# Scattering edge rows into a rank table: positions outside a pass go to spare rows by a clamp

## What is computed

```python
row = edge_index[0]                                   # src, 400000 node numbers
seg_sum = segment_sum(edge_attr, row, num_segments=N) # N = 12500, 32 features
seg_max = segment_max(edge_attr, row, num_segments=N)
cnt = segment_sum(ones, row, num_segments=N)
seg_mean = seg_sum / maximum(cnt, 1.0)
seg_max = where(cnt > 0, seg_max, 0.0)
h = concatenate([seg_sum, seg_max, seg_mean, u[batch]], axis=1)   # 97 columns
h = relu(h @ W1 + b1)                                 # 128 columns
x = x + (h @ W2 + b2)                                 # 64 columns
```

## Time and profile before

| | us |
|---|---|
| median of three runs (4393.61 to 4400.94) | 4397.47 |
| the profiled execution | 4387.55 |
| its span | 4385.8 |
| busy in the span: PE / DVE / ACT / POOL | 2956.9 / 2990.5 / 1416.7 / 3106.0 |

### The profile page before, as it was taken

How to read it: one execution, slowest core, us unless ns; L and a number is a source line. 1 busy time by engine, 2 the same in 40 slices (tenths; PEclk the granted TensorE clock), 3 DMA queues, 4 the chain that set the end, 5 groups by cost and what they waited for, 6 DMA issues and landing times.

```text
span 4385.8 us, 87474 instructions
## 1 busy us (share of the span) xinstructions
PE 2956.9 (67%) x18710; PEld 2189.1 (50%) x18710; DVE 2990.5 (68%) x12042; ACT 1416.7 (32%) x4649; POOL 3106.0 (71%) x3144
## 2 busy tenths in 40 slices
PE   5677667776666666666666677777777777677554
PEld 3455446654444444444444466666655555466443
DVE  7577559974444555545444589988888888589664
ACT  3333332233333333333333333333343333322133
POOL 5777777777777777777777777777677777777500
PEclk9987558855555555555555588877767787578677
DMA  7899873311111111111111233333313332143232
GB/s 294 315 379 372 326 261 113 113 25 26 25 26 26 25 26 26 26 25 26 25 25 26 65 112 100 102 110 99 99 53 90 87 96 83 42 119 118 71 98 69
DMA packets 410044, 454.47 MB, mean 104 GB/s; under 512 B 65002, under 2 KB 381460, under 8 KB 409620
## 3 DMA queue, kind: packets, MB, share of 16 engines
q1 hardware_dynamic: 309876, 401.37, 27.9%
q0 software_dynamic: 100000, 51.40, 4.8%
HBM read 221.50 MB, written 231.02 MB: 103 GB/s over the span
## 4 chain that ended last, share of the span: by engine, by line
POOL 43%; issue 21%; DVE 19%; DMA 7%; PE 6%; POOLq 2%; DVEq 1%; SPq 1%; ACT 1%; ACTq 0%
POOL sorted_rows L441 43%; DVE peak_ps L801 5%; DVE raised L784 3%; DMA sorted_rows<-edges,position 3%; DVE picked L725 3%; PE misc_ps L528 2%; DMA edges<-in_edge_attr 2%; DVE lent L717 2%; DMA win<-sorted_rows 1%; POOLq L441 1%; DVE hot_owner L708 1%; PE start_ps L497 1%; DVE raised L812 1%; DVE peak_ps L779 1%; DVE rank_c L735 1%
## 5 line engine op out<-in xcount | busy, mean ns | idle before, releaser
L441 POOL DMA_INDIRECT sorted_rows<-edges,position x3125 | 3083.6, 987 | 1022.3 <-issue 949.5
L501 PE MATMUL place_ps<-start_sb,lent 98*128 98x128 bf16 x3125 | 875.6, 280 | 1033.3 <-DVE rank_f L725 1031.3
L612 ACT ACTIVATE start_sb<-start_ps 98x128 bf16<-98x128 f32 x3125 | 865.7, 277 | 1663.9 <-PE start_ps L497 804.6
L497 PE MATMUL start_ps<-hot_owner,hot_block 128*98 128x128 bf16 x3125 | 977.9, 313 | 144.5 <-ACT start_sb L612 105.6
L725 DVE CUSTOM_DVE_ANT_0 picked<-place_ps,hot_owner 128x128 bf16<-128x128 f32 x3125 | 886.9, 284 | 99.9 <-issue 62.9
L501 PEld LDWEIGHTS place_ps<-start_sb,lent 98*128 98x128 bf16 x3125 | 375.2, 120 | 1149.7 <-DVE rank_f L725 1116.5
L503 PE MATMUL place_ps<-hot_owner,lent 128*128 128x128 bf16 x3125 | 892.6, 286 | 0.0
L740 DVE SCALAR_TENSOR_TENSOR position<-rank_c,src_f 128x5 int32<-128x5 f32 x625 | 104.6, 167 | 1079.0 <-DMA sorted_rows<-edges,position 1031.1
L497 PEld LDWEIGHTS start_ps<-hot_owner,hot_block 128*98 128x98 bf16 x3125 | 460.3, 147 | 621.3 <-ACT start_sb L612 611.1
L474 PE MATMUL same_ps<-lent 98*128 98x128 bf16 x3125 | 651.5, 287 | 78.0 <-DVE lent L717 38.0
L528 PE MATMUL misc_ps<-win,ident_f 128*128 128x224 f32 x2548 | 701.2, 438 | 0.0
(11 more groups left out here) (79 smaller groups left out, 1413.4 us busy)
## 6 DMA issues: line engine op xcount, KB each, us to landing
sorted_rows<-zeros SPq DMA_DIRECT2D x110, 1568.0 KB, 26.2
win<-sorted_rows SPq DMA_DIRECT2D x56, 1344.0 KB
edges<-in_edge_attr SPq DMA_DIRECT2D x625, 80.0 KB
sorted_rows<-edges,position POOLq DMA_INDIRECT x3125
win<-sorted_rows SPq DMA_DIRECT2D x28, 1008.0 KB
win<-sorted_rows SPq DMA_DIRECT2D x14, 1680.0 KB
win<-sorted_rows SPq DMA_DIRECT2D x14, 1568.0 KB
win<-sorted_rows SPq DMA_DIRECT2D x14, 896.0 KB
```

Source lines behind the costliest of these rows:

```text
L441: nc.gpsimd.indirect_dma_start(out=rows[:, :], out_offset=bass.IndirectOffsetOnAxis(ap=position[:, t:t + 1], axis=0), in_=edges[:, k, j * ...
L497: nc.tensor.matmul(start_ps[0:BLOCKS, 0:P], hot_block[:, t, :], hot_owner[:, t, :], start=False, stop=False, skip_group_check=True).then_i ...
L501: nc.tensor.matmul(place_slot(j), hot_block_t[:, slot, j * P:(j + 1) * P], start_sb[:, j, :], start=True, stop=False)
L612: nc.scalar.activation(start_sb[:, j, :], start_ps[0:BLOCKS, 0:P], ACT.Copy)\
```

## The change

The segments' planes are laid out with one spare plane ahead of, between and behind them: `BASE` starts at 1 and each segment takes one plane more. `shift` starts at `BASE[s]` and not at zero, so that the running count, and with it `rank_f`, is the plane's number and not the rank in the segment. `make_positions` limits that number from both sides, to the spare plane ahead of the segment and the one behind it, in one operation; the next multiplies by the plane's size, adds the node number and converts. The scatter has no bound any more. `take_counts` takes the base off again while it copies. The table has 112 planes in place of 110; the number of fills stays.

```diff
-BASE = [sum(s[1] for s in SEGMENTS[:k]) for k in range(len(SEGMENTS) + 1)]
+BASE = [1 + sum(s[1] + 1 for s in SEGMENTS[:k]) for k in range(len(SEGMENTS) + 1)]
...
-                nc.gpsimd.memset(shift[:, s, :], 0.0).then_inc(const_made, 1)
+                nc.gpsimd.memset(shift[:, s, :], float(BASE[s])).then_inc(const_made, 1)
...
                                     out_offset=bass.IndirectOffsetOnAxis(ap=position[:, t:t + 1], axis=0),
-                                    in_=edges[:, k, j * FEAT:(j + 1) * FEAT], in_offset=None,
-                                    bounds_check=(BASE[s] + ranks[s]) * PLANE - 1, oob_is_err=False)\
+                                    in_=edges[:, k, j * FEAT:(j + 1) * FEAT], in_offset=None)\
                                     .then_inc(edges_sent[k], 16)
...
-                    nc.vector.scalar_tensor_tensor(rank_c[:, mine], rank_f[:, mine], -float(ranks[s]), rank_f[:, mine],
-                                                   ALU.mult, ALU.max).then_inc(rank_clamped, 1)
-                    dve.wait_ge(rank_clamped, m * 2 + 1)
-                    nc.vector.tensor_scalar(rank_c[:, mine], rank_c[:, mine], float(ranks[s]), float(PLANE),
-                                            ALU.min, ALU.mult).then_inc(rank_clamped, 1)
-                    dve.wait_ge(rank_clamped, m * 2 + 2)
+                    nc.vector.tensor_scalar(rank_c[:, mine], rank_f[:, mine], float(BASE[s] + ranks[s]),
+                                            float(BASE[s] - 1), ALU.min, ALU.max).then_inc(rank_clamped, 1)
+                    dve.wait_ge(rank_clamped, m + 1)
                     if not begin:
                         dve.wait_ge(edges_sent[slot], c * (16 * GROUP))
-                    nc.vector.scalar_tensor_tensor(position[:, mine], rank_c[:, mine], float(BASE[s] * PLANE),
+                    nc.vector.scalar_tensor_tensor(position[:, mine], rank_c[:, mine], float(PLANE),
                                                    src_f[:, bass.ds(at * CHUNK + slot * GROUP, GROUP)],
-                                                   ALU.add, ALU.add).then_inc(position_ready, 1)
+                                                   ALU.mult, ALU.add).then_inc(position_ready, 1)
...
-                    nc.vector.tensor_copy(left_t[:, :], count_ps).then_inc(left_step, 1)
+                    nc.vector.tensor_scalar(left_t[:, :], count_ps, -float(BASE[s]), None, ALU.add).then_inc(left_step, 1)
```

## The result

The changed kernel takes 4322.59 us (median of 4, 4319.87 to 4331.62) against 4396.31 for the kernel before on the same chip: ratio 0.9835, 95% interval 0.9818 to 0.9852, so 73.7 us less. The forecast was 30 less; the time lies inside the stated range of 4130 to 4400 and far outside the forecast's own range of 4350 to 4388. The profiled execution took 4319.87 us, its span is 4318.1: 67.7 less than the span before.

A forecast was written before the change was run, and what follows sets the result against it. POOL's scatters were taken to bound the kernel, with DVE late in three stretches. 4387.55 - 30 (DVE) with 0 for bound and small things gives 4357.5; 9.9 for the median makes 4367 us, range 4130 to 4400 (own range 4350 to 4388).

The forecast's parts named there:

- What sets the time: Scatter stage: POOL paces alone at 1.282 us per scatter, except about 51 us of starvation where DVE is late.
- Step (1): DVE making positions: L732 goes, which counts only in the three late stretches; -30 us, at most 34.1.
- the 0.201 us per group: DVE time saved by dropping L732: 166 ns for the operation and 35 ns of idle time ahead of it.
- Rival C: Late stretches: PE and edge loads are as late as DVE, so the time stays at 4397 us; chance 0.08.
- Step (2): Scatter at L441 without its bound: register move gone for nothing, scatter's own 977 ns unchanged; taken as 0.
- a fixed walk over 128 rows: Scatter on POOL: reason for expecting no gain, its time supposedly set by building the transfer's entries.
- rival B: Scatter on POOL gets dearer without the bound, by 19 ns, giving 4409 us; 14 ns decides; chance 0.11.
- my own sign: Wrong if the quiet stretch's period leaves 1.28 us by over 1%, or starvation of 2560 to 3250 stays at 30.
- The register move: POOL's sequencer at L441: 3125 moves of 29 ns, 91 us, disappear but gain nothing, since the sequencer is ahead.
- Rival A: Scatter on POOL gets shorter without the comparison: 90 ns gives 4174 us, 45 ns gives 4273; chance 0.25.
- Step (3): Small things taken at 0: base subtracted in the count copy (1.6 us in all), shift's memset, two more planes, no added wait.

The follow-up runs named there:

- e2: Changed kernel with a bound on the scatter again, at the end of the spare plane: 4350.74 us, ratio 0.9921 to the kernel before.
- e4: Kernel before without L732, the clamp of negative ranks; bound and register move stay: 4353.16 us, ratio 0.9922 to the kernel before.
- e1: Kernel before with only the scatter's bound taken away: 4368.22 us, ratio 0.9951 to the kernel before.
- e7: Changed kernel, without bound, each scatter sending 64 of the 128 rows; only the scatter's duration was read: 892 ns, against 967 with 128 rows.
- e3: Changed kernel with a bound at the table's end, from a register set once before the loops: 4349.02 us, ratio 0.9920 to the kernel before.
- e5: Changed kernel with an unused register move written ahead of each scatter, no bound; the moves did not run: 4323.09 us.
- e6: Kernel before with the limiting operation at L735 writing another tile than the one it reads: 4386.66 us, ratio 1.0000 to the kernel before.
- e9: Changed kernel without edit on the second chip: 4321.23 us, ratio 0.9853 to the kernel before on that chip.
- e11: Changed kernel without any clamp, the operation at L731 removed too: 4317.21 us, ratio 0.9838 to the kernel before.

## Why the prediction was wrong

**What sets the time: right.** POOL's 3125 scatters, each with a constant 0.305 us of idle time, paced the stage, and three late stretches starved for 51 us. Time was gained in both, in the scatter's own duration and in starvation.

**Step (1), DVE's operation: right in mechanism, the size a little low.** It was taken as -30, at most -34. Alone it gives 39 to 44 us of starvation and 37 to 46 us of the stage (e2 to e4). In the changed kernel starvation falls by 32.8 us only, because faster scatters starve sooner (e1: 51 to 54); that the fall of the idle time, 31.8 us, came out so near 30 is partly luck. The term that was too small is the 0.201 us per group: the 52 ns by which the next operation became shorter were not in it. I had the row with 225 ns for L735 beside 171 for its middle value within reach and didn't ask why mean and middle differ. Rival C (the 0.2 us are swallowed) is refuted: starvation of 2533 to 3195 fell from 30.9 to 8.9.

**Step (2), the bound: this is the step that failed.** "I take 0" stood against a measured 10 ns per scatter, and 3125 x 10 = 31 us is as much as the whole forecast. The reason given for it, that the shortest scatter takes 975 ns and the middle one 977, shows that the time is steady, not what it is made of: without the bound it is about as steady, 962 and 967. And "a fixed walk over 128 rows" is wrong by e7, at least as a walk row by row. The rows of comparison were wrong in kind as well: memset and select on 128 columns led me to think of a price per row, between 0 and 90 ns, and to choose an end. A price of 10 ns per instruction is near that end, but I had worked out in rival B that 14 ns per scatter were worth the whole forecast, so 0 needed a better reason than this one.

Nor would my own sign have shown the miss: I was to be wrong if the period left 1.28 us by more than 1%, and it went from 1.282 to 1.272, by 0.8%. Only the mean in the quiet stretch shows it, 970 ns where I had 975 to 982. That the time lies inside 4130 to 4400 says little, since that range was made to reach from A to C.

The Trainium skill, page "GPSIMD Engine Reference", section "Performance pitfalls for Q7 kernels", gives cycles per element for compare and select, and the estimate worked out from them was 110 to 216 ns. The runs show 10 ns, at 64 and at 128 rows, and the measurement decides. The Trainium skill, page "DMA: Bandwidth & Descriptors", section "Anatomy of one DMA", says that many descriptors can be emitted before their incremental cost shows. The runs agree in that twice the rows cost 75 ns more on 892. The 977 ns that the prediction set against this page are the whole scatter on POOL; no row splits off the generation of descriptors.

**The register move: right.** e2 and e3 differ in it and tie; e5, which was to show it without the bound, did not run it. **Rival A** had the right place with 90 ns in place of 10, **rival B** the wrong sign. **Step (3): right** as far as can be told; e4, which has none of these parts, is 2.4 us from e2.

**Of the 72.8 us of the stage in the profile after**, some 33 are starvation (51 to 18), 31 the bound. The rest, some 9 us of busy time, lies mostly in the few scatters that take much longer than the middle one, and its size differs between profiles of one kernel: 974 and 976 ns on average for the changed kernel, 3043.8 and 3050.3 us. Over five profiles with the bound (before, e2, e3, e4, e6) the scatters are busy for 3083.5 us on average, over five without (changed kernel, e1, e5, e9, e11) for 3050.2: 33 us, 10.7 ns per scatter. So most of those 9 us belong to the one profile and to neither part.

## What to carry to other kernels

Where one instruction runs thousands of times back to back and paces the kernel, no term per instruction may be put at zero without a reason that bears on it: multiply first (here 10 ns is 31 us). The middle of wide bounds is no better: 45 ns, worked out under rival A, gave 4273 us, further from the measured 4323 than 4367 is. What settles such a price is one run with the term taken away (e1), and a sign of being wrong that is finer than the term. To see whether a price is per instruction or per row, halve the rows and look at the one duration. Look in the trace whether an added instruction ran at all (e5). And compare parts by the time of the stage that they change, since the end of this kernel varied by 10 us.

## What the runs showed of the hardware that was not expected

An indirect scatter's time on POOL changes little with its rows: 892 ns for 64, 967 for 128, and 0.305 us between two scatters in either case. A bound adds 10 ns at both counts. An operation on 5 columns of DVE (170 ns) took about 400 in 144 of 625 cases when another short DVE operation with two inputs ran right ahead of it, and in none when that was gone. One such case in the kernel before, in order of time (start, duration):

```profile
841.27 1.25 POOL L441 DMA_INDIRECT sorted_rows<-edges,position  x1 [0.30 <-issue]
...
841.91 0.16 DVE L732 SCALAR_TENSOR_TENSOR rank_c<-rank_f 128x5 f32<-128x5 f32 x1
842.10 0.40 DVE L735 TENSOR_SCALAR rank_c<-rank_c 128x5 f32<-128x5 f32 x1
```

The scatter beside it is longer too (1.25 us for 0.98), and both end within 0.02 us of each other. All 144 cases are like this in time: each starts 0.51 us or more after the start of a scatter and ends within 0.01 us of that scatter's end. The other 481 start earlier, between scatters, or so late that they outlast the scatter (28), and none of them takes over 0.23 us. In the changed kernel 112 clamps start as late in a scatter, and none takes over 0.18 us. So the long case needs both, L732 right ahead and the later part of a scatter beside it. What the two wait for in common is open: e4 and e6 exclude the multiply and working in place.

And the end of the kernel moves with PE's granted clock near it. In the two profiles at 0.58 (e1, e11) what follows the start of the last scatter takes 256.0 and 253.9 us; in the other eight profiles with all 128 rows, at 0.66 to 0.77, it takes 243.5 to 247.3. What decides the clock there was not tried.
